# Windowed attention layers: scores, mask and the values of the pair before in one stretch of 64 by 32 tiles, and new engine orders

## The reference

```python
qkv = x @ Wqkv                                  # 128 -> 3 * 1024, 16 heads of 64
q, k = l2norm(q) * qs, l2norm(k) * ksc          # then rotary factors
mask = (it < jb) | (it > jb + w) | (jb == -1)   # windows of w = 32 queries, 64 keys
attn = softmax(where(mask, -max, q @ k.T * 8))  # per window and head
x = x + (attn @ v) @ Wo
x = x + (a * gelu(gate)) @ W2 + b2              # a, gate = layernorm(x) @ W1 + b1
```

## Time and profile before

| what | value |
|---|---|
| median of 3 runs | 3897.81 us (3894.65 to 3899.23) |
| the profiled execution's own time | 3900.27 us |
| its span (first to last instruction) | 3898.5 us |
| mean granted PE clock | 0.980 |
| busy: PE / PEld / DVE / ACT / POOL | 95% / 65% / 83% / 74% / 79% |
| the loop of 90 pairs | from about 839 us to about 3760 us |

### The profile page before, as it was taken

One profiled execution on the slowest core, in us unless ns is written; L12 is line 12 of the kernel. 1 busy time (PEld: TensorE's weight loads), 2 busy tenths in 40 slices (PEclk: granted clock), 3 DMA queues, 4 the chain that ended last, 5 costly groups with the idle time before them and its releaser, 6 DMA issues. The chain is left out here.

```text
span 3898.5 us, 173964 instructions
## 1 busy us (share of the span) xinstructions
PE 3697.8 (95%) x65792; PEld 2516.8 (65%) x65792; DVE 3220.9 (83%) x6438; ACT 2893.9 (74%) x5873; POOL 3065.0 (79%) x3927
## 2 busy tenths in 40 slices
PE   4899997899999999999999999999999999999997
PEld 2344443577777777777777777777777777777775
DVE  7787884788888888888888888888888888888885
ACT  5466665677777777777777777777777777777774
POOL 4211111889999999999999999999999999999993
PEclk7799998999999999999999999999999999999998
DMA  2422211222222322223222232222232222222222
GB/s 78 75 38 38 38 26 34 80 67 65 65 65 70 87 63 63 64 63 91 64 64 65 65 85 72 65 65 65 65 91 62 64 63 63 74 64 65 65 66 56
DMA packets 176134, 250.64 MB, mean 64 GB/s; under 512 B 46726, under 2 KB 65796, under 8 KB 175108
## 3 DMA queue, kind: packets, MB, share of 16 engines
q1 hardware_dynamic: 176004, 248.94, 26.1%
HBM read 39.08 MB, written 8.39 MB: 12 GB/s over the span
## 5 line engine op out<-in xcount | busy, mean ns | idle before, releaser
L1075 PE MATMUL w_ring<-w_wqkv,w_xs 128*128 (+1 forms) x2304 | 1155.5, 604 | 23.3 <-DMA w_scales<-in_L_ffn_k_scale 19.1
L1466 POOL TENSOR_TENSOR w_qr<-w_raw,w_tc 128x512 f32<-128x512 f32 x384 | 490.4, 1277 | 163.9 <-PE w_ring L1095 157.3
L1480 POOL TENSOR_TENSOR w_qr<-w_qr,w_qrot 128x512 f32<-128x512 f32 x384 | 573.1, 1492 | 0.0
L1075 PEld LDWEIGHTS w_ring<-w_wqkv,w_xs 128*128 128x128 f32 x2304 | 378.2, 191 | 189.3 <-issue 161.1
L1473 POOL TENSOR_TENSOR w_qrot<-w_raw,w_tc 128x512 f32<-128x512 f32 x384 | 486.3, 1278 | 0.0
L1151 PEld LDWEIGHTS w_ring<-w_pts,w_vw 64*64 64x64 f32 x24576 | 378.4, 135 | 96.2 <-issue 96.2
L669 DVE TENSOR_REDUCE a_row_max<-a_ring 128x1 f32<-128x512 f32 (+3 forms) x608 | 361.4, 655 | 87.1 <-PE a_ring L485 62.3
L1266 ACT ACTIVATE w_ksq<-w_ring 128x512 f32<-128x512 f32 x384 | 229.5, 598 | 273.1 <-PE w_ring L1075 273.1
L598 ACT ACTIVATE a_probs<-a_wide 128x512 f32<-128x512 f32 (+1 forms) x608 | 313.8, 582 | 157.3 <-PE a_wide L506 154.7
L638 POOL TENSOR_SCALAR_AFFINE_SELECT a_probs<-a_probs 128x512 f32<-128x512 f32 x128 | 81.6, 638 | 437.2 <-ACT a_probs L598 437.2
L1151 PE MATMUL w_ring<-w_pts,w_vw 64*64 64x32 f32 x24576 | 400.1, 220 | 7.1 <-issue 5.5
(11 more groups left out here) (158 smaller groups left out, 8649.8 us busy)
## 6 DMA issues: line engine op xcount, KB each, us to landing
w_vw<-w_v SPq DMA_DIRECT2D x1152, 128.0 KB, 2.3
w_vw<-w_v SPq DMA_DIRECT2D x768, 64.0 KB, 2.0
a_q_stack<-q_parts SPq DMA_DIRECT2D x144, 64.0 KB
a_k_stack<-k_parts SPq DMA_DIRECT2D x144, 64.0 KB
w_wqkv<-in_L_ffn_Wqkv SPq DMA_DIRECT2D x6, 1536.0 KB, 6.0
q_parts<-ap_parts SPq DMA_DIRECT2D x8, 384.0 KB, 3.5
k_parts<-ap_parts SPq DMA_DIRECT2D x8, 384.0 KB, 3.4
w_wo<-in_L_ffn_Wo SPq DMA_DIRECT2D x12, 256.0 KB, 3.2
```

The source lines that it names most:

```text
L1075: nc.tensor.matmul(bank(what, i, u)[:], xs[u][:], rhs, start=True, stop=True).then_inc(done, 1)
L1466: nc.gpsimd.tensor_tensor(by_head(qr[i][:]), by_head(raw[i][:]), wide(table(u, Q_COS)), ALU.mult).then_inc(q_straight[i], 1)
L1480: nc.gpsimd.tensor_tensor(qr[i][:], qr[i][:], qrot[i][:], ALU.add).then_inc(q_added[i], 1)
```

## The change

1. **One stretch.** `scores` and `values` go; `block(r, u)` takes their place. It issues the mask of (r, u) as eight bf16 products, one per 64 by 32 tile, and then, for j = 0 to 7, eight value products of (r-1, u), eight score products of (r, u), eight value products. Values are cut into halves of 32 features, so 128 products of 64 by 32 tiles instead of 64 of 64 by 64. The values are now those of one pair before the scores in the same call.
2. **Mask rows.** The mask is kept once (`mask_bf`), and 32 columns that select its rows take the place of the identity. For the first window of a sequence `sel_first` is written for each pair by a new operation on ACT, `choose_rows`.
3. **Carry and floor on ACT.** `carry` moves from POOL to ACT as two activations per pair; the floor of `refine` moves to ACT behind `factor_log`.
4. **Orders.** All `body` lists and `USES` are new. The feed-forward part lags one pair more. SP loads the feed-forward weights of a layer two window groups later.

```diff
-        mask_bf = sb("mask_bf", [P, PAIRS_B, 512], BF16)
-        ident_bf = sb("ident_bf", [P, P], BF16)
+        mask_bf = sb("mask_bf", [P, 512], BF16)
+        sel = sb("sel", [P, BAND], BF16)
+        sel_both = sb("sel_both", [P, BAND], BF16)
+        sel_first = sb("sel_first", [P, BAND], BF16)
...
-            def scores(r, u):
...
-            def values(r, u):
...
+            def block(r, u):
...
+                def mask():
+                    for w in range(4):
+                        for e in range(2):
+                            d = slice(HD * e, HD * (e + 1))
+                            chosen = sel_first if u == 0 and w == 0 else sel
+                            nc.tensor.matmul(bank("sc", e, u)[BAND * w:BAND * (w + 1), :], chosen[d, :], mask_bf[d, :],
+                                             start=True, stop=False, skip_group_check=True)
+
+                def score(j):
+                    for w in range(4):
+                        for e in range(2):
+                            rows, d = slice(BAND * w, BAND * (w + 1)), slice(HD * e, HD * (e + 1))
+                            mm = nc.tensor.matmul(bank("sc", e, u)[rows, WIN * j:WIN * (j + 1)], qt[u][d, j, rows],
+                                                  kt[u][d, j, BAND * w:BAND * w + WIN], start=False, stop=True, skip_group_check=True)
+                    return mm
+
+                def value(n, w):
+                    for e in range(2):
+                        for half in range(2):
+                            for par in range(2):
+                                keys, at = slice(HD * par, HD * (par + 1)), 256 * e + HD * n + BAND * half
+                                rows = slice(HD * e + BAND * half, HD * e + BAND * (half + 1))
+                                mm = nc.tensor.matmul(bank("ct", par, u)[rows, P * n + BAND * w:P * n + BAND * (w + 1)],
+                                                      vw[u][keys, w, at:at + BAND], pts[e][keys, n, BAND * w:BAND * (w + 1)],
+                                                      start=True, stop=True)
+                    return mm
+
+                if has_scores:
+                    mask()
+                for j in range(8):
+                    if has_values:
+                        mm = value(j // 2, 2 * (j % 2))
+                    if has_scores:
+                        sm = score(j)
+                        if j == 7:
+                            sm.then_inc(scored, 1)
+                    if has_values:
+                        mm = value(j // 2, 2 * (j % 2) + 1)
...
             def body(pair):
-                scores(pair - 3, 0)
...
-                values(pair - 4, 1)
...
+                block(pair - 3, 0)
...
+                block(pair - 3, 1)
...
                 nc.scalar.activation(lnv[:], over[:], ACT.Ln, bias=tiny[:, 0:1]).then_inc(logged, 1)
+                nc.scalar.activation(ssc[:], over[:], ACT.Identity, bias=tiny[:, 0:1]).then_inc(floored, 1)
...
+            def choose_rows(r):
...
+                nc.scalar.activation(sel_first[:], sel_both[:], ACT.Copy, scale=first[:, bass.ds(r % PAIRS_B, 1)]).then_inc(sel_ready, 1)
...
+            def carry(r, u):
...
+                nc.scalar.activation(kt[u][:, :, 0:BAND], kt[1 - u][:, :, P:KEYS], ACT.Copy, scale=factor).then_inc(carried, 1)
...
-                nc.gpsimd.tensor_tensor(ssc[:], over[:], tiny[:], ALU.add).then_inc(chain, 1)
```

More of the change, by code:

```diff
@@ L897, in windowed @@
         LAG = 6
[L900 removed]
[6 rows of a table removed]
+        USES = (("sc", 0, 0, 3), ("sc", 1, 0, 3), ("ct", 0, 0, 4), ("ct", 1, 0, 4), ("pt", 0, 1, 4), ("k", 1, 0, 2),
[5 rows of a table added]
+                ("hid", 0, -1, 5), ("hid", 1, -1, 5), ("q", 0, 0, 1), ("hid", 2, -1, 5))
         assert len(USES) % len(ring) == 0
@@ L1046, in layer_loads @@
                     load_early(layer + 1, (layer + 1) % 2)
-                with sp.Fori(2, PAIRS) as r:
+                windows(first + 2, 0)
+                windows(first + 2, 1)
+                fixed_wait(sp)
+                sp.wait_ge(xa_ready, first + PAIRS)
+                load_ffn(layer)
+                with sp.Fori(3, PAIRS) as r:
                     windows(first + r, 0)
@@ L1096, in turn_q @@
                 mm.then_inc(q_flipped[i], 1)
-            def scores(r, u):
[L1100 to L1112, removed]
-                chunk(pe, carried, r, u)
-                for j in range(HEADS // 2):
-                    for w in range(4):
-                        for e in range(2):
-                            rows, d = slice(BAND * w, BAND * (w + 1)), slice(HD * e, HD * (e + 1))
-                            mm = nc.tensor.matmul(bank("sc", e, u)[rows, WIN * j:WIN * (j + 1)], qt[u][d, j, rows],
-                                                  kt[u][d, j, BAND * w:BAND * w + WIN], start=False, stop=True, skip_group_check=True)
-                mm.then_inc(scored, 1)
             def turn_p(r, u, e):
@@ L1324, in store_kt @@
                                bank("kt", i, u)[:].rearrange("p (j n) -> p j n", j=4)).then_inc(k_stored[i], 1)
+            def carry(r, u):
+                if outside(r):
+                    return
+                for i in range(2):
+                    chunk(act, k_stored[i], r, u, back=1)
+                factor = keep[:, bass.ds(r % PAIRS_B, 1)] if u == 0 else 1.0
+                nc.scalar.activation(kt[u][:, :, 0:BAND], kt[1 - u][:, :, P:KEYS], ACT.Copy, scale=factor).then_inc(carried, 1)
             def store_qt(r, u, i):
@@ new lines, in body @@
+                store_p(pair - 3, 1, 0)
+                copy_q(pair - 1, 0, 1)
+                carry(pair - 2, 1)
+                store_kt(pair - 2, 1, 1)
+                copy_v(pair - 2, 1, 0)
+                choose_rows(pair - 1)
+                exps(pair - 2, 0, 1)
+                square_k(pair - 1, 0, 0)
+                store_qt(pair - 2, 1, 1)
+                store_kt(pair - 2, 1, 0)
+                build_xs(pair - 1, 1)
+                copy_v(pair - 2, 1, 1)
+                store_qt(pair - 2, 1, 0)
@@ new lines, in body @@
+                sum_k(pair - 2, 0, 1)
+                add_ffn(pair - 6)
+                sum_q(pair - 2, 0, 0)
+                rotate_k(pair - 2, 0, 0)
+                straight_k(pair - 2, 0, 0)
+                sum_k(pair - 2, 0, 0)
+                add_k(pair - 2, 0, 0)
+                add_attention(pair - 4, 0)
+                sum_p(pair - 3, 0, 1)
+                sum_p(pair - 3, 0, 0)
+                invert(pair - 3, 0, 1)
+                divide(pair - 3, 0, 1)
+                max_scores(pair - 3, 1, 1)
@@ L1838, in shape_constants @@
     seen = (j >= i % BAND) & (j <= i % BAND + BAND)
-    seen_first = seen & ((i >= BAND) | (j >= BAND))
-    masks = np.stack([np.where(m, f(0.0), f(MASKED)) for m in (seen_first, seen)], 1).astype(f)
+    row = i % WIN
+    mask = np.where(row < BAND, np.where(seen, f(0.0), f(MASKED)), np.where(j < BAND, f(MASKED), f(0.0)))
+    rows = np.concatenate([np.ones((P, 1)), np.where(row < BAND, 1.0, 0.0)], 1)
+    masks = np.concatenate([mask, np.where(i % BAND == np.arange(BAND)[None, :], 1.0, 0.0), rows], 1).astype(f)
     later = np.where(np.arange(P)[None, :] > np.arange(P)[:, None], f(MASKED), f(0.0)).astype(f)
```

266 lines of the change are left out of this document (123 added, 143 removed), and 11 rows, old and new, of the table USES.

## The result

| | before | after |
|---|---|---|
| median time | 3,898.5 us | 5,411.7 us (5,404.0 to 5,417.8) |
| ratio | | 1.388 (95% interval 1.387 to 1.390) |
| profiled span | 3,898.5 us | 5,402.2 us |
| mean granted TensorE clock | 0.980 | 0.859 |

The change costs 1,513 us; the prediction said 919. It is slower for the reason forecast, and outside the forecast's range.

What follows compares the result with a forecast made beforehand. PE's instruction list bounds the kernel; 5.35 + 4.55 - 0.3 = 9.6 us a turn, +864 over 90 turns, and +55 outside the loop give 4,817 us. Ends 4,334 and 5,285; about 8 in 10 for 4,010 to 5,250.

Steps and rivals of the forecast that it cites:

- a store of eight: PE's instruction store, assumed to hold 8 packets, loses all in each turn, as 9 would have to be kept.
- price of a packet: Time per missing instruction packet inside a dense PE stretch: 3.5 us, ends 2.67 and 3.69.
- the first stretch: Mixed stretch at the loop's head: four missing packets, 14.3 us before cover, 9.3 against 3.95 now, +5.35 a turn.
- the second stretch: The turn's later mixed stretch: two packets waited for, 8.5 us, +4.55 a turn.
- outside the loop: 14 more stretches at 4.95 us each, +69, less stops already there: +55 us.
- five table loads: ACT gains three table loads of 1.283 us a turn, hidden under a PE of 42 us: cost 0.
- cover of 5.0 us at the turn: Large products still queued on PE at the loop's turn hide part of the first stretch's 14.3 us, leaving 9.3.
- 0.3 counted: Gain from fewer mode changes on PE, four stretches of small tiles becoming two: -0.3 us a turn, between 0 and 0.42.
- the layer's wait: Later feed-forward weight loads on SP meet a feed-forward part that itself runs a pair later: cost 0.
- (a): Rival: packets are kept in the loop and the pass rate stays, +0.8 us a turn, 4,025 us; chance 0.11.
- (b): Rival: packets kept and mixed passes faster, 8.5 ns each, -1.1 us a turn, 3,824 us; chance 0.07.
- (c): Rival: only the packet at the loop's turn is lost, 2.1 us a turn on top of (a), 4,214 us; chance 0.06.

Runs made afterwards that it cites:

- e2: The change with the last two value steps of each block in whole tiles, 1,751 instructions a turn, seven packets touched; 4,344.1 us, ratio 1.114.
- e3: e2 with 33 more instructions ahead of the loop, so the same loop touches eight packets; 5,122.9 us, ratio 1.314.
- e8: The change with the last ten calls of PE's loop moved to its head, so it turns between large products, still eight packets touched; 5,602.8 us, ratio 1.438.
- e5: e1 with the third GELU of a pair moved right behind the second on ACT, to save table loads; 3,917.3 us, ratio 1.005.
- e14: e5 with feed-forward biases and norm vectors loaded a layer ahead, two q stores earlier on ACT, and add_k ahead of sum_k on VectorE; 3,793.1 us, ratio 0.973.
- e7: The change itself with the third GELU moved right behind the second on ACT; 5,365.3 us, ratio 1.376.
- e6: e2 with the third GELU moved right behind the second on ACT; 4,025.8 us, ratio 1.033.
- e1: The change with all scores issued first, then values in whole 64 by 64 tiles, 1,367 instructions a turn; 4,270.0 us, ratio 1.095.

## Why the prediction was wrong

**Right.** The mechanism: q8 in each turn with nine packets (9.0 counted); a store of eight, which was assumed as a power of two and which e2 and e3 bear out, but for the turns of e3 that keep their packets; price of a packet 3.5 us (3.47, 3.74 and 3.48 from one stop to the next); three stops in the first stretch (one of them only 0.77 us), one ahead of it, two in the second; the second stretch from 2006.86 to 2015.22, 8.4 us, predicted 8.5; PE's busy share 76%, predicted near 75; outside the loop 1,513 - 1,448 = 65 us, predicted 55 (the 14 us taken off there for stops were too much, show 7.9); five table loads, none ending a wait of PE in the change.

**Wrong: a mean turn of 48.9 us, predicted 42.4.** That is 585 of the 595 us by which the time was missed. The 6.5 us come from:

1. *The cover of 5.0 us at the turn.* This is the step that failed. The 5.0 us were my guess at how much work PE still has queued when its sequencer reaches the turn. No run shows them; what the runs show in their place is 1.6 and 1.7 us. The two L1226 passes of 2028.47 are done with 0.43 us later, so the stretch could begin at 2028.9. From there to its end (2041.58) it took 12.7 us, where 14.3 - 5.0 = 9.3 was predicted: the cover was 14.3 - 12.7 = 1.6 us. My lower bound, from the stops at the turn of the first layer, was 3.5 - 2.35 = 1.2 us and had a row behind it; the 5.0 came from none. **+3.4 us.** e8 shows the same size another way: its stop at the turn, between large products, is 1.84 us, which leaves 3.5 - 1.84 = 1.7 us of cover. What sets the size of the cover the runs do not show.
2. *The work outside the stretches.* In the turn shown it is 47.6 - 12.7 - 8.4 = 26.5 us; predicted were 32.8 - 2 x 3.95 - 0.3 = 24.6. **+1.9 us.** The largest part is *the clock, which the sum did not have*: in and behind the stretches it falls to 0.50, and large products take longer: 1.75 - 1.12 for two, 2.87 - 1.88 for four (1.88 is what four take in e5), 1.11 - 0.66 for four transposes, and 0.69 - 0.44 for the two of xf (0.44 in e14), about +2.3 us, read off single rows; no run took the clock away. The mask that waits for the bank which w_kr frees adds 0.4 (the [0.42 <-DVE w_kr] above; e14 takes it away), where I had counted the new orders at nothing. Against these the new orders save more than the 0.3 counted: in e14, which has no such waits, 31.4 less two stretches of 3.6 us as in e5 leaves 24.2. These make 2.3 where 1.9 were found, which is as near as single rows go.
3. *The turns that are longer than the one shown.* The mean lies 1.3 us above it. **+1.3 us.** About half is the layer's wait, costed at 0 as hidden: the two turns of 52 and 54 us at the start of each layer make 0.6 to 0.7 of the mean. The rest lies in the turns of about 50 us, and what makes them longer was not looked into.
4. The second stretch, -0.1.

*The table loads*, costed at 0 too, are 46 us in e7, 0.5 us a turn at most; which of these parts they lie in no row shows.

**Rivals.** (a), (b) and (c) fell with the packets. Parts of them can be judged: (a) put a turn with kept packets at 33.6 us; e2, near to that case, has 37.1, and e6, the same without three of the loads, 33.5. The sentence that under a PE of 33 us ACT's loads would be a rival was right and too mild: they cost 353 us at an ACT that is busy for 83%, since they stand in a chain and the clock falls behind the waits (to 0.50 in e1). The condition of (b), a pass under 10.0 ns, is met (9.3), and yet eight mixed steps come out slower than whole values by the estimate from the rows of e5 and e6 (3.8 and 3.60 us); the comparison should have been with the same order unmixed, 3.60 us, not with the 3.95 of the earlier trace rows.

**Where the 1,513 us go,** by the chain of kernels: the new orders with whole values and two table loads +19 (e5: the mask -37, the layer's wait +34, the two late releases +47 and +43, which leaves -68 for scores and values in one block and the rest of the new orders, if the parts simply add up; the passes are no faster there, since the 3.60 us of a stretch and the 3.95 before differ by the mask's 0.3); three table loads +353 (e1); six mixed steps +74 (e2); eight packets touched instead of seven +779 (e3); the last two mixed steps and the loss of the packets in every turn +289. The shares depend on the order in which the steps are taken: with two table loads, from e6 to e7, the packets and the last two steps are 1,340 us, and the three loads are the 46 that are left.

## What to carry to other kernels

Before a loop body grows, count its instructions on PE, with waits and weight loads, and the packets that it touches from where it starts: in this kernel a turn of 1,879 instructions fetched 9.0 packets each time where one of 1,349 fetched none, and at the edge 33 instructions ahead of the loop decided 779 us. Where small passes come at a pace of their own (9.3 to 15.6 ns apart here), cutting them into more of them must be weighed against that pace. On ScalarE count table loads on the chain, not in the busy share (353 us in e1, with ACT busy for 83%); and take the cover of a stall from a row that shows one (1.6 us here), not from an idea of how much is queued (5.0).

## What the runs showed of the hardware

- 33 instructions ahead of a loop of 1,751 cost 779 us (e2, e3). At that edge the turns of one run take from 35.6 to 54.0 us (e3, 900 to 3800 us).
- The granted clock was 0.50 for 3.4 and 10.2 us of a turn of the change, behind stops of 0.8 to 2.8 us, and 0.50 in e1 behind two waits of 1.26 us; in e14, without stops, its mean is 1.00 from 900 to 3600 us of the loop.
- Passes on 64 by 32 tiles, scores and values in turn, start 9.3 ns apart on average (e6), passes of scores alone 11.0 and of values on 64 by 64 tiles 15.6; eight bf16 masks on eight tiles take 0.22 us where two on the whole array took 0.54.
- Where the loop turns, PE stops for 1.84 us even between large products (e8).
